# A decoder layer ordered by a planner: one buffer fill moved ahead of the first statistics, big loads held until W_q and W_k are there, new durations and a new order

## The reference

```
x = x + attn(layernorm(x), Wq, bq, Wk, bk, Wv, bv, Wo, bo)        # 16 heads of 16, causal, ALiBi
h = layernorm(x)
x = x + softmax(h @ ctx^T / 16 masked by mask_BxS2) @ ctx          # ctx: 16 x 64 x 256
w_up, w_down = each rounded to FP4 values with one power-of-two scale per block of 32
x = x + gelu(layernorm(x) @ w_up + b_up) @ w_down + b_down         # 256 -> 1024 -> 256
```

## Time and profile before

| | us |
|---|---|
| median of 3 runs | 143.77 |
| lowest, highest | 143.28, 144.34 |
| the profiled execution | 142.73 |
| its span, first to last instruction | 140.9 |
| busy in that span: PE, DVE, ACT, POOL | 117.4, 109.8, 94.8, 61.9 |

### The profile page before, as it was taken

One profiled execution on the slowest core, in us unless ns is written; L12 is line 12 of the kernel. 1 busy time (PEld: TensorE's weight loads), 2 busy tenths in 40 slices (PEclk: granted clock), 3 DMA queues, 4 the chain that ended last, 5 costly groups with the idle time before them and its releaser, 6 DMA issues.

```text
span 140.9 us, 3182 instructions
## 1 busy us (share of the span) xinstructions
PE 117.4 (83%) x1046; PEld 84.5 (60%) x1046; DVE 109.8 (78%) x253; ACT 94.8 (67%) x212; POOL 61.9 (44%) x108
## 2 busy tenths in 40 slices
PE   0035999869898997998999899798999679999991
PEld 0014743627634466775767678567787259899970
DVE  0758489999999999999999999977664595664642
ACT  2123347656776776667668876679995699999970
POOL 7565349305450045446477884526543085000000
PEclk9999999999999999999999999999999999999999
DMA  4899999970000000000000000000000200020202
GB/s 144 269 348 329 368 302 334 353 239 1 2 5 0 2 0 5 0 0 0 5 0 7 0 0 0 5 0 2 5 0 0 74 0 0 5 77 0 81 0 74
DMA packets 8864, 10.70 MB, mean 76 GB/s; under 512 B 1648, under 2 KB 7920, under 8 KB 8720
## 3 DMA queue, kind: packets, MB, share of 16 engines
q1 hardware_dynamic: 7760, 9.64, 21.1%
q10 hardware_dynamic: 1088, 0.86, 2.0%
HBM read 9.45 MB, written 1.05 MB: 74 GB/s over the span
## 4 chain that ended last, share of the span: by engine, by line
PE 40%; DVE 26%; issue 11%; DMA 11%; ACT 4%; POOL 4%; SPq 1%; DVEq 1%; ACTq 0%
PE bank L1100 10%; PE bank L1116 10%; DMA x_sb<-in_x_dram 6%; DMA raw_T<-in_W_down_T_dram 4%; DVE s_sb L805 4%; DVE s_max L810 4%; DVE k L781 3%; PE bank L1023 3%; PE bank L958 3%; PE bank L983 3%; PE bank L1050 2%; PE bank L1039 2%; DVE stats L758 2%; PE bank L971 2%; POOL rstd L560 2%
## 5 line engine op out<-in xcount | busy, mean ns | idle before, releaser
L592 POOL TENSOR_TENSOR s_sb<-s_sb,s_max 128x512 f32<-128x512 f32 x16 | 18.0, 1127 | 25.8 <-DVE s_max L810 25.8
L928 DVE TENSOR_TENSOR h_lo<-h_sb,h_hi 128x256 fp32r<-128x256 f32 x32 | 14.2, 442 | 10.9 <-ACT h_sb L726 10.7
L958 PE MATMUL bank<-const,xn 128*128 128x128 f32 x48 | 11.0, 319 | 12.9 <-DVE xn L767 10.8
L1100 PE MATMUL bank<-xn_T,w_up_q 128*128 128x256 f16 x128 | 19.4, 274 | 0.7 <-ACT h_sb L726 0.7
L1116 PE MATMUL bank<-w_down_q,h_hi 128*128 128x256 f32 x64 | 18.9, 320 | 0.5 <-DVE h_lo L928 0.2
L726 ACT ACTIVATE h_hi<-bank,bias_cols 128x256 fp32r<-128x256 f32 x32 | 15.4, 481 | 1.9 <-issue 0.4
L1116 PE MATMUL bank<-w_down_q,h_lo 128*128 128x256 f32 x64 | 16.5, 281 | 0.0
L560 POOL TENSOR_TENSOR rstd<-var_eps,minus_half 128x1 f32<-128x1 f32 x24 | 14.8, 617 | 2.0
L958 PEld LDWEIGHTS bank<-const,xn 128*128 128x128 f32 x48 | 5.9, 155 | 16.2 <-issue 8.9
L726 ACT ACTIVATE h_sb<-bank,bias_cols 128x256 f32<-128x256 f32 x32 | 15.4, 481 | 0.0
L971 PE MATMUL bank<-xn_T,w_T 128*128 128x512 f32 x32 | 15.1, 611 | 0.1
(11 more groups left out here) (86 smaller groups left out, 265.2 us busy)
## 6 DMA issues: line engine op xcount, KB each, us to landing
raw_T<-in_W_up_T_dram SPq DMA_DIRECT2D x1, 1024.0 KB, 10.3
raw<-in_W_up_dram SPq DMA_DIRECT2D x1, 1024.0 KB, 12.7
ctx_T<-in_ctx_by_feature_dram SPq DMA_DIRECT2D x1, 1024.0 KB, 7.1
ctx_sb<-in_ctx_dram SPq DMA_DIRECT2D x1, 1024.0 KB, 9.4
raw_T<-in_W_down_T_dram SPq DMA_DIRECT2D x1, 1024.0 KB, 6.3
raw<-in_W_down_dram SPq DMA_DIRECT2D x1, 1024.0 KB, 8.3
out_dram<-x_sb SPq DMA_DIRECT2D x8, 128.0 KB, 1.8
x_sb<-in_x_dram SPq DMA_DIRECT2D x4, 128.0 KB, 3.6
```

The source lines that it names most:

```text
L592: pool.tensor_tensor(tile, tile, s_max[:, u % S_RING, :].unsqueeze(2).broadcast_to([P, HC, S]), ALU.subtract).then_inc(centred, 1)
L928: dve.tensor_tensor(h_lo[:, i % H_RING, :], h_sb[:, i % GELU_RING, :], h_hi[:, i % H_RING, :].bitcast(F32), ALU.subtract).then_inc(split_r ...
L958: last = pe.transpose(dst[:, c * P:(c + 1) * P], xn[:, ring[t % len(ring)], c * P:(c + 1) * P], ident)
L1100: last = pe.matmul(dst[:, 0:GN], w_up_q[:, c, f * P:(f + 1) * P], xn_T16[:, g * GT:(g + 1) * GT, at16:at16 + P], start=(k == 0), stop=(k = ...
```

## The change

Instructions are the same ones with the same shapes and the same number. What moves:

1. `v2_zero` is one stage for half 0 on POOL and `v2_zero2` one for half 1 on DVE. Every LN1 `stats` now comes behind `v2_zero2` in the list, so DVE's memset (L786, L789) is issued first of all DVE work.
2. SP waits for `qk_loaded` instead of `v_loaded` before the ALiBi table and all loads behind it.
3. The planner's durations are recalibrated (among them the loads), and it now stretches a DVE stage of the kinds in `TWO_PORT` by part of the overlap with a POOL stage of the kinds in `STREAMS`.
4. `URGENCY`, `DRIFT` and `PATIENCE` are a new set of numbers, so the order on every engine is a new one.

```diff
-        add("stats", (n, t), "dve", 0.55, before)
-        add("rstd", (n, t), "pool", 1.1 if n in NORM_ON_ACT else 0.85, [("stats", (n, t))])
+        add("stats", (n, t), "dve", 0.55, before + ([("v2_zero2", ())] if n == LN1 else []))
+        add("rstd", (n, t), "pool", 1.18 if n in NORM_ON_ACT else 0.85, [("stats", (n, t))])
...
-    loads = (("load_x", (0,), 2.0), ("load_x", (1,), 0.4), ("load_x", (2,), 0.4), ("load_x", (3,), 0.4),
-             ("load_v", (), 0.9), ("load_x", (HALF,), 1.5), ("load_biases", (), 0.1), ("load_qk", (), 1.5),
-             ("load_alibi", (), 1.5), ("load_rows", (), 0.4), ("load_blocks", (), 3.0), ("load_weights", (), 3.0),
-             ("load_row_biases", (), 0.8), ("load_o", (), 0.8), ("load_mask", (), 0.3), ("load_ctx", (), 6.0))
+    loads = (("load_x", (0,), 2.0), ("load_x", (1,), 0.2), ("load_x", (2,), 0.2), ("load_x", (3,), 0.2),
+             ("load_v", (), 0.8), ("load_x", (HALF,), 1.4), ("load_biases", (), 0.1), ("load_qk", (), 1.3),
+             ("load_alibi", (), 2.3), ("load_rows", (), 0.2), ("load_blocks", (), 2.8), ("load_weights", (), 2.8),
+             ("load_row_biases", (), 0.6), ("load_o", (), 0.6), ("load_mask", (), 0.1), ("load_ctx", (), 5.8))
...
+    add("v2_zero", (), "pool", 2.5)
+    add("v2_zero2", (), "dve", 1.6)
...
-        add("v2_zero", (h,), ("pool", "dve")[h], 2.5)
...
 URGENCY = {
-    "attn_turn": 278, "v_odd": 164, "quant": 142, "pv": 129, "load_o": 60, "normalise": 58, "spread": 55,
-    "gelu": 51, "out_proj": 43, "x_table": 38, "load_rows": 37, "x_scale": 33, "split": 32, "v_even": 31,
...
+    "attn_turn": 220, "normalise": 199, "quant": 142, "x_max": 63, "k_copy": 51, "qk_bias": 51, "rstd": 51,
+    "add_down": 50, "stats": 35, "x1": 30, "v_even": 29, "load_blocks": 28, "k": 28, "add": 28, "x_prob_T": 27,
+    "q_round": 26, "pv": 23, "up": 23, "load_up": 21, "x_mask": 21, "final": 20, "amax": 20, "load_rows": 18,
...
+    "spread": -30, "valid": -37, "x_scale": -38, "x_fill": -38, "load_v": -39, "norm": -41, "prob_T": -44,
+    "store": -46, "split": -47, "scale_T": -47, "prob_copy": -65, "exp": -71, "k_rest": -72, "binade": -72,
+    "q_inverse": -73, "v": -84,
 }
...
 PATIENCE = {
-    "dve": 0.1, "pe": 0.1, "pool": 0.04, "act": 0.0,
+    "pool": 0.58, "dve": 0.14, "act": 0.08, "pe": 0.0,
 }
...
+        if engine == "dve" and key[0] in TWO_PORT and streaming > start:
+            us += min(STRETCH * us, 0.6 * (streaming - start))
+        if engine == "pool" and key[0] in STREAMS:
+            streaming = start + us
...
-            sp.wait_ge(v_loaded, 16)
+            sp.wait_ge(qk_loaded, 16)
             sp.dma_start(alibi_sb[:, :, :], alibi).then_inc(alibi_loaded, 16)
...
-                if stage == "v2_zero" and at[0] == 1:
+                if stage == "v2_zero2":
                     dve.memset(v2[:, B // 2:B, :, :, :], 0.0).then_inc(v2_zeroed[1], 1)
```

More of the change, by code:

```diff
@@ L79, in layer_norm @@
         ring = XN_RING[n]
[L80 to L81 removed]
+        add("stats", (n, t), "dve", 0.55, before + ([("v2_zero2", ())] if n == LN1 else []))
+        add("rstd", (n, t), "pool", 1.18 if n in NORM_ON_ACT else 0.85, [("stats", (n, t))])
         reused = [("turn", (n, t - len(ring)))] if t >= len(ring) else []
[L83 removed]
+        add("norm", (n, t), "act" if n in NORM_ON_ACT else "dve", 0.49 if n in NORM_ON_ACT else 0.32, [("rstd", (n, t))] + reused)
         last = ("low", (t,)) if n == LN3 else ("turn_copy", (n, t))
@@ L211 @@
 ACT_TABLE_US = 1.3
+STREAMS = ("centre", "add_bo", "add_down", "v2_zero", "x_fill", "max", "round")
+TWO_PORT = ("norm", "k_rest", "binade", "q_cut", "q_inverse", "q_exponent", "q_step", "q_clip", "x_table")
+STRETCH = 1.1
 PE_WINDOW_US = 3.413
@@ L217 @@
 URGENCY = {
-    "attn_turn": 278, "v_odd": 164, "quant": 142, "pv": 129, "load_o": 60, "normalise": 58, "spread": 55,
-    "gelu": 51, "out_proj": 43, "x_table": 38, "load_rows": 37, "x_scale": 33, "split": 32, "v_even": 31,
-    "load_x": 29, "load_row_biases": 28, "load_blocks": 28, "x1": 28, "scale_copy": 25, "x_scores": 22,
-    "load_up": 21, "x_mask": 21, "load_qk": 20, "load_alibi": 20, "k_rest": 19, "spread_copy": 18, "v_own": 16,
-    "final": 15, "stats": 14, "q_cut": 13, "max": 12, "q_round": 12, "v_move": 11, "v_copy": 9, "v_spread": 9,
@@ L223 @@
-    "amax": 8, "store": 8, "add_bo": 7, "load_vo": 6, "attn_copy": 6, "x_prob_copy": 5, "k": 5, "q": 5,
-    "q_clip": 5, "x_prob_T": -5, "low": -5, "x_max": -5, "add_down": -7, "add": -9, "prob_copy": -9,
-    "q_exponent": -9, "k_copy": -11, "k_flat": -12, "q_inverse": -13, "q_divide": -14, "load_weights": -14,
-    "load_ctx": -16, "norm": -16, "q_out": -17, "x2": -19, "up": -19, "scores": -23, "q_add": -25,
-    "binade": -27, "valid": -29, "qk_bias": -32, "scale_T": -34, "v2_zero": -35, "reload": -36, "x_fill": -37,
@@ L228 @@
-    "centre": -38, "rows_copy": -38, "rstd": -40, "load_biases": -41, "down": -42, "q_copy": -42,
-    "load_mask": -43, "load_v": -45, "x_read": -47, "q_step": -48, "exp": -48, "x_exp": -60, "prob_T": -87,
-    "turn": -87, "v": -142,
+    "attn_turn": 220, "normalise": 199, "quant": 142, "x_max": 63, "k_copy": 51, "qk_bias": 51, "rstd": 51,
+    "add_down": 50, "stats": 35, "x1": 30, "v_even": 29, "load_blocks": 28, "k": 28, "add": 28, "x_prob_T": 27,
+    "q_round": 26, "pv": 23, "up": 23, "load_up": 21, "x_mask": 21, "final": 20, "amax": 20, "load_rows": 18,
@@ new lines @@
+    "load_mask": 17, "v_own": 16, "scores": 16, "centre": 14, "q_divide": 12, "x_exp": 12, "v_move": 11,
+    "x_read": 11, "turn": 11, "v_copy": 9, "v_spread": 9, "load_row_biases": 7, "turn_copy": 7, "load_vo": 6,
+    "attn_copy": 6, "load_o": 4, "gelu": 3, "load_x": 3, "scale_copy": 2, "out_proj": 1, "load_alibi": 1,
+    "x_prob_copy": 1, "q_step": 1, "q_exponent": -1, "load_biases": -2, "rows_copy": -3, "x_table": -4,
+    "add_bo": -5, "q_copy": -5, "q_clip": -10, "reload": -11, "x_scores": -12, "max": -13, "down": -13,
@@ L236 @@
-    "x_prob_T": 10.0, "turn": 9.5, "spread_copy": 6.8, "add_bo": 6.8, "x_mask": 6.4, "out_proj": 6.4,
-    "x_scale": 6.0, "max": 4.8, "pv": 4.0, "q_clip": 3.2, "v_spread": 3.2, "prob_T": 3.0, "attn_turn": 2.6,
-    "up": 2.0, "q": 1.6, "prob_copy": 1.4, "scores": 1.2, "attn_copy": 1.2, "rstd": 0.6, "down": -0.2,
-    "stats": -0.3, "split": -0.4, "x_exp": -0.8, "spread": -1.2, "scale_T": -2.1, "k_flat": -2.4, "x1": -2.4,
-    "x_scores": -2.8, "q_add": -3.2, "normalise": -3.8, "centre": -4.0, "norm": -4.7, "add_down": -7.6,
@@ L241 @@
-    "turn_copy": -9.3, "v_even": -9.6, "scale_copy": -10.7, "final": -11.2, "v_odd": -13.6, "q_step": -16.0,
-    "q_inverse": -20.8, "store": -23.2, "v_move": -24.0, "q_exponent": -99.2,
+    "q_out": 85.6, "v2_zero": 48.0, "v_odd": 39.2, "scores": 27.2, "q_exponent": 24.0, "k_rest": 20.8,
+    "x_prob_copy": 19.2, "k_copy": 16.0, "q_round": 16.0, "v_copy": 12.0, "turn": 10.2, "store": 7.2,
+    "x_mask": 6.4, "spread": 6.0, "x_scores": 6.0, "gelu": 3.5, "low": 3.2, "v_spread": 3.2, "split": 2.8,
@@ new lines @@
+    "centre": 2.6, "x1": 2.0, "x2": 2.0, "k_flat": 1.6, "turn_copy": 1.6, "stats": 1.4, "attn_turn": 1.0,
+    "x_prob_T": 0.8, "out_proj": 0.8, "load_x": 0.6, "down": 0.5, "prob_T": 0.4, "up": -1.4, "pv": -1.6,
+    "q_copy": -1.6, "x_exp": -2.0, "spread_copy": -2.8, "normalise": -3.0, "scale_T": -3.2, "add_down": -4.0,
+    "add": -4.2, "add_bo": -5.6, "final": -6.0, "k": -6.4, "q_step": -8.0, "amax": -10.4, "exp": -10.8,
+    "q_clip": -11.2, "q_add": -12.8, "v": -12.8, "q_inverse": -16.0, "v_move": -24.0, "q_cut": -30.4,
@@ L283, in schedule @@
     pe_used = {}
+    streaming = 0.0
     while ready:
@@ L565, in _ @@
                                            ALU.mult, ALU.mult).then_inc(shift_ready[n], 1)
-                if stage == "v2_zero" and at[0] == 0:
+                if stage == "v2_zero":
                     pool.memset(v2[:, 0:B // 2, :, :, :], 0.0).then_inc(v2_zeroed[0], 1)
```

25 lines of the change are left out of this document (13 added, 12 removed).

## The result

| | before | changed |
|---|---|---|
| median, us | 143.53 | 149.09 |
| lowest, highest | 141.53, 144.34 | 146.57, 150.02 |
| profiled execution, its span | 142.73, 140.9 | 150.02, 148.2 |
| busy PE, DVE, ACT, POOL | 117.4, 109.8, 94.8, 61.9 | 122.3, 110.6, 94.5, 64.4 |
| granted TensorE clock, mean | 1.00 | 0.94 |

The ratio of the changed kernel to the one before is 1.034, 95% interval 1.025 to 1.042. Faster by 2.7 us was forecast, within 138.4 to 145.0; the time lies above that range.

A forecast was written before the change was run, and what follows sets the result against it. DVE was taken as nearly full from 29.9 to 93.45 us and PE from 113.06 to 135.70, behind a waiting start. Start 1.7 plus durations 1.0 give 2.7 us: 143.77 to 141.1 us, range 138.4 to 145.0.

The forecast's parts named there:

- The start: Stretch before the first projection: it would start at 15.9 instead of 17.59, a gain of 1.7 us.
- The hold: SP's later wait: the 0.81 MB left at 6.00 take 2.2 us, so tiles 4 to 7 land at about 8.2.
- It does not do what it says: Loads before SP's wait stay slow: tiles 4 to 7 at 10.0, start 15.3 to 17.7; within the absorbed case's 0.24.
- Priced at nothing: DVE's `amax` wait for W_up transposed, landing at 17.2, falls into idle time: cost nothing, about 1 at the late bound.
- What is late next: Loads behind SP's wait issue 3.8 us later; rows table lands at 13.9, W_up transposed at 17.2 against 15.9.
- the start gain is absorbed: DVE, now earlier, meets later loads of ALiBi, W_up and W_down; 1.7 or 1.0 us lost, median 142.9; chance 0.24.
- signs of being wrong: DVE waits on DMA over 1.5 us between 16 and 30, DVE idle over 4 us between 30 and 90, or extra ACT table loads.
- The slower one: `rows_copy` holds ACT's queue ahead of the copies of tiles 2 and 3: 145.2 us and more; chance 0.16.
- The rows table early: Rows table lands near 11.9, `rows_copy` hides under `v` (0, 0), projection starts at 14.6: 139.8 us; chance 0.12.
- The tail repacked with fewer loads of ACT's table: In the tail ACT does all exps before the first gelu, saving two table loads: 139.0 us; chance 0.10.
- the durations: Recalibrated planner durations bring fewer DVE and POOL collisions, as in `amax_floor` and `binade`: 1.0 us gain.
- PE and DVE both run nearly full from there on: From the first projection on, both engines are nearly full, so the sum is made for the projection's start time.

The follow-up runs named there:

- `fill_first`: The kernel before in its old order, with DVE's memset ahead of the first statistics and `x_fill` behind the last `rstd` of the first layer norm: 143.13 us, ratio 1.000.
- the fillers: The changed kernel with 20 additional matmuls, whose results nothing reads, in five gaps of TensorE: 144.88 us, ratio 1.015 to the kernel before.
- the table early: The changed kernel with the context loads behind the W_down reloads and the rows table issued ahead of SP's wait: 140.94 us, ratio 0.985 to the kernel before.

## Why the prediction was wrong

**The start: right in place, in size partly by luck.** The forecast was 15.9 for the first projection and a gain of 1.7; it was 15.63 and 2.0. Errors cancelled on the way. Tile 3's statistics ran at 7.04 instead of 6.75, but `norm` 0, which I had put behind them by misreading the order, came before them, at 5.65; so `v` (0, 0) was on time. The rows table was issued 1.1 us later than worked out and took 4.5 us instead of 5.3; so it was there at 14.2. And the 2.0 us came without the hold's help, since the new order without it starts the projection at 15.39. The memset did cost 0.45 us at the first statistics, and nothing in all: `fill_first` is at 1.000.

**The hold: ended too early in the sum.** I let the last 0.81 MB ahead of the hold move at 369 GB/s, a rate that the earlier trace rows shows for a stretch in which the big loads were already queued. Without them the core moved 215 GB/s from 6.00 to 9.63. The hold ended 1.1 us later than forecast. The rival "It does not do what it says" had taken 200 GB/s and 10.0 for tiles 4 to 7; with 215 and 9.63 it was the nearer one, and it asked for a start of 15.3 to 17.7. The Trainium skill, "DMA: Bandwidth & Descriptors", section "Anatomy of one DMA", was cited as speaking against holding loads back. That section gives its 2 us and 436 GB/s for loads that GpSimd issues; SP and ACT issue all loads here. What the traces show is in the cited direction: slice 3 at 102 GB/s, and every load behind the hold issued later, up to the context. As a price it falls short: the same 1 MB of W_down transposed took 4.9, 6.3, 8.1 and 11.4 us, and 2 us plus its bytes over 436 GB/s is 4.4 (an estimate by that section).

**"Priced at nothing": the step that failed.** In "What is late next" the delay of 3.8 us was followed to the rows table and to W_up transposed, and priced at nothing behind them. The two cost waits of 0.45 us on ACT and 1.6 on DVE (1.62 before 17.03), the second in idle time as said. It was not followed through to the end of SP's queue. Behind W_up stand the masks and the context, and behind the context, at a time set by DVE, the reload of W_down transposed. Its issue hardly moved, 22.84 and 22.89. The context ahead of it moved from 16.62 and 17.10 to 17.71 and 18.19, and ran on beside it, so that it landed at 31.0 instead of 29.2, while all of DVE's work ahead of its first `amax` was done at 28.4 instead of 29.0. Before, the two met to within 0.2 us. These 0.2, the 0.6 by which DVE came sooner and the 1.8 by which the load came later make the 2.6. The rival "the start gain is absorbed" named this wait, and the earlier trace rows showed how full DVE was behind it, but its price was capped at what the start had gained. The runs show 2.6 us in the new order and 4.1 in the old, more than the gain, because the start's gain itself adds to the wait: DVE comes sooner, the bytes come later. With the two context loads behind the reloads, and no other edit, the wait is gone and the ratio goes from 1.034 to 0.986. The prediction's own signs of being wrong, a wait of DVE on a DMA of over 1.5 us between 16 and 30 and over 4 us of DVE idle between 30 and 90, both came: 2.6 us, and 8.1 of 60.

**The clock: not in the sum at all.** The forecast took PE's rate as given, since the granted clock was 1.00 in the profile before. With the fillers, PE's clock stayed up through both stretches and the median fell by 4 us. That part is shown. That DVE's wait brings the clock down is not. For it: of the four profiles with a wait of over 2 us and no fillers, three have the lower clock somewhere between 31 and 57 us (the changed kernel, the hold alone, and the new order without the hold, at 41 to 45), and none of the nine with a wait of 0.7 us or less has it between 21 and 89. Against it: the profile has PE of the changed kernel busy in all of the 2.60 us in which DVE waited, and its clock fell only 12 us later, right behind 1.07 us of waiting for `binade`; and the later falls, at 90 us and beyond, come with the wait and without it. What brings the clock down stays open. The Trainium skill, "TensorE: Matmul & The Clock Gate", section "Part 1: The HAM clock gate", says that how busy TensorE has been recently decides between 1.2 and 2.4 GHz. The traces agree in part: the stretch at 0.51 comes behind one with 10.00 us busy of 12.20. But PE was then busy all of 13.80 us before the clock came back, and the kernel before kept 1.00 over 6.42 of 8.54 us.

**The rivals.** The slower one put `rows_copy` in ACT's queue: right place for the start's 1.0 us, and no part of the loss that a run shows (0.985 against 0.986 with the table early). The rows table early: wrong, as it landed at 14.2 and not near 11.9, and `rows_copy` had a second thing to wait for. The tail repacked with fewer loads of ACT's table: wrong, there are three as in the earlier trace rows.

**The gain of 2.7 us: not there even without the loss.** With the same swap, and so with no wait, the new order is at 140.64 and 141.09 us and the old at 142.38, 1.3 to 1.7 us apart; at full clock the spans are 138.6 to 139.3 against 139.8. That is the start and the durations together, for which the sum had 1.7 + 1.0. The start's part is the doubtful one: its step "PE and DVE both run nearly full from there on" let every us of the start through, while in the old order a projection 1.6 us sooner brought nothing. For the durations 1.0 us was taken; `binade` took 196 ns both times in the changed kernel instead of 650 and 1034, but 0.60 us at 27.64 in the swapped one. These three long `binade` steps ran while POOL was in a TENSOR_TENSOR (22.76 to 25.90 and 34.23 to 35.27 before, 26.59 to 28.19 with the swap), the two of 196 ns just after one had ended (28.05 and 42.28), so the collisions are real, but the new order avoids them only in some executions. No run parts the two terms.

**What the sum comes to.** The new order with the swap, at full clock: 139.2. Wait of DVE: 2.6. Half clock: about 17 us in the profiled execution. Its price per us comes from executions of one kernel: with the swap 3.3 us in 12.0 and 4.8 in 14.4 (142.5 and 144.0 against 139.2; the time at half clock is worked out from the mean clock), about 0.3 for each, and without the hold 6.3 in 14.2 and 6.4 in 17.4 (145.3 and 145.4 against 139.0), about 0.4. So 5 to 7 us, and 147 to 149 together, against 148.2. But at 0.3 the sum falls short in six of the changed kernel's eight executions, most where the clock hardly fell: at a mean clock of 0.988 it gives 142.9 and the span was 146.1. The split between wait and clock is therefore good to about 3 us, and some of the loss may be neither.
